# Operand slots of two sweeps, and the places of combining, norm and split, in a graph layer on one core

## The chip, the core and the metric

One NeuronCore of a Trainium2 chip runs the whole program. Time is device microseconds of one execution, as the median of three runs. The engines are TensorE (PE; PEld is its weight loading), VectorE (DVE), ScalarE (ACT), GpSimd (POOL) and SyncE (SP), which issues most DMAs. Each engine takes its instructions in the order in which they are written; semaphores join the engines.

## The reference, cut to what matters

There are 6250 nodes with 512 features and 106250 edges (50000 random pairs in both directions and a loop on each node), sorted by destination.

```python
Q = relu(x @ Wq + bq); V = x @ Wv + bv
Q = relu(layer_norm(Q)); H = sum(Q, axis=1) ** 2; H = pi / (2 * m) * H      # m from max(H) - min(H)
cosQ, sinQ = Q * cos(H), Q * sin(H)
out  = cosQ @ (cosQ.T @ V) + sinQ @ (sinQ.T @ V)
norm = cosQ @ sum(cosQ, 0) + sinQ @ sum(sinQ, 0) + EPS
gcn  = segment_sum((x @ Wg)[src] * coef, dst) + bg
y = relu(layer_norm(out / norm + gcn + V) * gamma + beta)
x = layernorm(x + y)
```

## The kernel before, in words

Nodes are cut into 49 tiles of 128 rows (`TILES`; the last, number `FULL` = 48, has 106). The program has two parts. In the first (up to about 345 us) PE multiplies every tile by Wg, and a table of rows for the graph part is written to DRAM. The second part is one list of 882 steps (`STEPS` = 49 x 18), which every engine walks with `for q in range(...)`. It is a schedule by hand: the functions `qv_at`, `cos_at`, `sin_at` and `out_at` give the step at which a tile of a stage begins, and each engine puts its share of the tile at a fixed distance `at` from there. The engines hold no common clock: an engine may be some steps ahead of another, as far as semaphores let it.

Each step holds one chunk of the graph part: POOL gathers 128 table rows by an indirect DMA (L532, a ring of 9 buffers; the gather of chunk n waits until PE is done with chunk n-9), DVE makes a 128x128 one-hot matrix (L1013, 6 buffers; it waits for the landed rows and for PE's chunk n-6), and PE multiplies the two into a bank (L1373 and L1375, the two halves of the rows). A destination tile has 18 steps; `k` is the step within it. At its end `end_tile` (L1390) announces the sum; `combine_tile` on DVE (L1043, at k = 1) adds it to the buffer `combine`; `store_combined` on ACT (L676, k = 3) writes that to DRAM; `combine_load` on SP (L415, k = 8) brings the next tile's V into the same buffer, to which `add_own` (L1023 and L1025, k = 16) adds the node's own row.

Beside the chunks run four stages, one after the other:

1. Steps 0 to 206: Q and V of 37 tiles, one tile in 6 steps. PE multiplies (L1252 to L1254: each product is made of three matmuls of high and low parts); DVE adds the biases (`v_keep` L935 at 4, `q_bias` L940 at 7) and takes the variance (L947).
2. Steps 214 to 376, the cosine sweep: cosQ.T @ V over all 49 tiles, one in 10/3 steps, summed in four banks. For tile g, ACT rounds the high parts (`m_round`: L686 for Q, L688 for V), DVE subtracts to get the low parts (`m_split`: L1094 and L1095), and PE multiplies (`m_step`). The four operands lie in a slot of the tile `operands`; there are two slots, `g % 2`, and two buffers for V's rows.
3. Steps 383 to 529, the sine sweep, one tile in 3 steps, in the same way; g runs on from 49.
4. Steps 536 to 877, the output stage, one tile in 7 steps: PE transposes Q of the next tile and multiplies it by the moments (`out_step`: products at 0 to 5, the norm sums L1491 and L1492 at 0 to 2); DVE splits the next tile's transposed Q (`o_split`, L1124) and takes the norm (`o_norm`, L1133 to L1138), both at 3, then `o_mix` (L1155, L1157) at 8, `o_affine` (L1165 to L1169) at 11, `o_factors` (L1177, L1178) at 14; ACT does `o_round` at 3, roots (L704, L707) at 10 and 13 and the last scaling (L713) at 16. Seven steps make one period, so `at` 8 stands at place 1 of the next tile's period, 11 at place 4 and 14 at place 0.

In a step DVE's one-hot stands first and the stage's work after it. PE has the opposite order:

```python
# DVE                                   # PE
chunk(seq, k)                           m_step(...) / out_step(n, at)
combine_tile(seq - 1)   # if k == 1     chunk(seq, k)
m_split(...) / o_norm(...) / o_mix(...)
```

A semaphore wait of tile n is written `done(n)`; `freed(n, 2)` is the wait for tile n-2.

## Time and profile before

| | |
|---|---|
| median of 3 runs | 1703.74 us (1702.14 to 1708.99) |
| profiled execution | 1704.63 us, its span 1702.7 us |
| PE busy | 1534.5 us (90%) |
| DVE busy | 1087.7 us (64%) |
| ACT, POOL busy | 625.4 us (37%), 922.0 us (54%) |
| granted TensorE clock, mean | 0.982 |
| DMA | 423.86 MB, 249 GB/s in the mean |

(A step of PE ends with its chunk.) Busy time is the sum of the instructions' spans on an engine. In the second part PE has no long pause; what the mean of 90% hides is where its many short pauses lie, and that is read stage by stage.

### The profile page before, as it was taken

The numbers are of one execution on the slowest core, as the hardware profiler recorded it, in microseconds if no ns is written. First come the engines' busy times: TensorE is split into PE (matmuls) and PEld (weight loads), VectorE is DVE, ScalarE is ACT, GpSimd is POOL, SyncE is SP. The second block draws the span as 40 slices with busy tenths as digits, with TensorE's granted clock in tenths as the row PEclk, the third lists the DMA queues.
The fourth block names the chain that finished last, engine by engine and source line by source line (L and its number), as shares of the span: only waits on it lengthen the run. The fifth ranks groups of instructions, "written<-read, shape, count | busy, mean of one in ns | idle before, by whom it ended". The sixth has DMA issues, their size and how long they took to land.

```text
span 1702.7 us, 24721 instructions
## 1 busy us (share of the span) xinstructions
PE 1534.5 (90%) x7715; PEld 1026.3 (60%) x7715; DVE 1087.7 (64%) x3259; ACT 625.4 (37%) x1419; POOL 922.0 (54%) x1026
## 2 busy tenths in 40 slices
PE   5788999899999898999998999989999999889995
PEld 3566777666556554655554655556666666656663
DVE  6999665655555455555555555556777777667765
ACT  5999876521212112222222222222333333233322
POOL 0000000166666666777776777776666666666662
PEclk9999999999999998999998999999999999999998
DMA  6444444698999888888787888888888888788884
GB/s 224 143 149 166 145 170 148 215 299 289 296 297 297 284 288 264 263 267 262 251 272 229 280 252 273 261 257 269 273 277 283 285 280 284 236 279 273 275 256 146
DMA packets 172757, 423.86 MB, mean 249 GB/s; under 512 B 24143, under 2 KB 25803, under 8 KB 172617
## 3 DMA queue, kind: packets, MB, share of 16 engines
q0 software_dynamic: 71120, 236.74, 45.9%
q1 hardware_dynamic: 79980, 146.16, 25.1%
q10 hardware_dynamic: 21516, 39.29, 6.0%
q8 instruction: 64, 1.05, 0.2%
q14 instruction: 77, 0.62, 0.1%
HBM read 351.42 MB, written 70.67 MB: 248 GB/s over the span
## 4 chain that ended last, share of the span: by engine, by line
PE 57%; DVE 19%; issue 10%; ACT 5%; another core or an unknown queue 3%; DMA 3%; POOL 2%; DVEq 0%; POOLq 0%; ACTq 0%; SPq 0%
PE bank L1252 12%; PE bank L1254 11%; PE bank L1253 11%; PE bank L1373 9%; PE bank L1375 8%; DVE stage L919 3%; DVE one_hot L1013 2%; DVE stage L915 2%; PE bank L1298 2%; POOL gathered L532 2%; DMA gathered<-scaled_g,index_slots 1%; DVE operands L928 1%; DVE stage L1166 1%; PE bank L1492 1%
## 5 line engine op out<-in xcount | busy, mean ns | idle before, releaser
L532 POOL DMA_INDIRECT gathered<-scaled_g,index_slots x882 | 885.6, 1004 | 420.8 <-issue 211.4
L1373 PE MATMUL bank<-gathered,one_hot 128*128 128x512 f16 x882 | 348.1, 395 | 93.8 <-DVE one_hot L1013 55.1
L1252 PE MATMUL bank<-weights,operands 128*128 128x512 f32 x784 | 396.8, 506 | 8.8 <-DVE stage L935 7.1
L1375 PE MATMUL bank<-gathered,one_hot 128*128 128x512 f16 x882 | 340.3, 386 | 0.0
L1013 DVE TENSOR_SCALAR one_hot<-iota_bf,dst_in_tile,gathered 128x128 bf16<-128x128 bf16 x882 | 257.2, 331 | 120.8 <-DMA gathered<-scaled_g,index_slots 64.5
L1253 PE MATMUL bank<-weights,operands 128*128 128x512 f32 x784 | 311.7, 398 | 0.0
L1254 PE MATMUL bank<-weights,operands 128*128 128x512 f32 x784 | 310.3, 396 | 0.0
L1373 PEld LDWEIGHTS bank<-gathered,one_hot 128*128 128x128 bf16 x882 | 85.4, 97 | 300.0 <-issue 210.8
L1252 PE MATMUL bank<-operands 128*128 128x512 f32 x392 | 198.8, 507 | 0.0
L1252 PEld LDWEIGHTS bank<-weights,operands 128*128 128x128 f32 x784 | 149.4, 191 | 72.3 <-DVE stage L935 8.8
L704 ACT ACTIVATE operands<-stage,stats 128x512 fp32r<-128x512 f32 x98 | 70.8, 723 | 328.7 <-DVE stats L1143 201.7
L517 POOL COPY dst_slots<-dst_cols 128x18 f32 x49 | 11.1, 226 | 327.0 <-issue 326.5
L686 ACT CAST operands<-nodes 128x512 fp32r<-128x512 f32 x98 | 60.7, 619 | 332.1 <-PE bank L1254 143.5
L1094 DVE TENSOR_TENSOR operands<-nodes,operands 128x512 fp32r<-128x512 f32 x98 | 68.0, 694 | 179.0 <-issue 123.3
L1254 PEld LDWEIGHTS bank<-weights,operands 128*128 128x128 f32 x784 | 148.1, 189 | 36.5
L1253 PEld LDWEIGHTS bank<-weights,operands 128*128 128x128 f32 x784 | 149.7, 191 | 22.2
L1254 PE MATMUL bank<-operands 128*128 128x512 f32 x392 | 155.2, 396 | 0.0
L1253 PE MATMUL bank<-operands 128*128 128x512 f32 x392 | 154.0, 393 | 0.0
L602 ACT ACTIVATE stage<-iota_bf,combine 128x128 bf16<-128x128 bf16 x372 | 115.8, 391 | 8.2 <-DVE combine L808 6.3
L1252 PEld LDWEIGHTS bank<-operands 128*128 128x128 f32 x392 | 74.5, 190 | 44.2 <-issue 6.0
L1375 PEld LDWEIGHTS bank<-gathered,one_hot 128*128 128x128 bf16 x882 | 88.4, 100 | 11.6 <-issue 4.0
L623 ACT ACTIVATE nodes<-nodes,stats 128x512 f32<-128x512 f32 x49 | 39.8, 812 | 142.1 <-issue 96.6
(219 smaller groups left out, 2228.0 us busy)
## 6 DMA issues: line engine op xcount, KB each, us to landing
stage<-values SPq DMA_DIRECT2D x98, 256.0 KB
stage<-in_x SPq DMA_DIRECT2D x96, 256.0 KB, 2.7
turned_x<-operands SPq DMA_DIRECT2D x37, 512.0 KB, 3.2
operands<-turned_x SPq DMA_DIRECT2D x37, 512.0 KB
gathered<-scaled_g,index_slots POOLq DMA_INDIRECT x882
scaled_g<-pairs SPq DMA_DIRECT2D x49, 260.0 KB, 2.1
pairs<-scaled_g SPq DMA_DIRECT2D x49, 260.0 KB
values<-stage ACTq DMA_DIRECT2D x49, 256.0 KB
```

Of the source, the lines that this page charges most:

```text
L532: pool.indirect_dma_start(out=plain(row_ring[k % RING]), out_offset=None, in_=table, in_offset=bass.IndirectOffsetOnAxis(ap=index_slots[:, ...
L602: last = act.activation(mod_hot[b % 2][:, HOTS + n, :], iota_bf[:, :], ACT.Sign, bias=column(stair_edge, b * STAIRS + n))
L686: act.copy(f_hi, q_tile(t))
L704: act.activation(operands[:, 5 + n % 2, :], stage[:, 2 + j, :], ACT.Square, bias=st[:, 1:2], accum_out=st[:, 2:3]).then_inc(s[f"o_squared{ ...
L919: last = dve.tensor_scalar(mod_hot[half][:, c, :], iota_bf[:, :], column(dst_mod, c0 + c), None, ALU.is_equal)
L1013: dve.tensor_scalar(one_hot[:, k % HOT, :], iota_bf[:, :], column(dst_in_tile, seq % 2 * PER_TILE + k), scale_of(row), ALU.is_equal, ALU.m ...
L1094: dve.tensor_tensor(f_lo, q_tile(t), plain(f_hi), ALU.subtract)
L1252: pe.matmul(out_ap, a_hi, b_hi, start=start and n == 0, stop=False, skip_group_check=True)
L1253: pe.matmul(out_ap, a_hi, b_lo, start=False, stop=False, skip_group_check=True)
L1254: last = pe.matmul(out_ap, a_lo, b_hi, start=False, stop=stop and n == len(pairs) - 1, skip_group_check=True)
L1373: pe.matmul(gcn_banks[seq % 2][:, :], one_hot[:, k % HOT, :], hi, start=k == 0, stop=False, skip_group_check=True)
L1375: pe.matmul(gcn_banks[seq % 2][:, :], one_hot[:, k % HOT, :], lo, start=False, stop=False, skip_group_check=True).then_inc(s["chunk_summed ...
```

## The change

Both sweeps get four operand slots, `g % 4`. Slots 2 and 3 lie in `weights[:, 2]` and `weights[:, 3]`, where V's weights stood, which no product reads after the first stage. The rows of V for them land in `pairs[:, 1]` and `pairs[:, 2]`. ACT and DVE prepare a tile two tiles ahead of PE instead of one, and SP loads V three ahead. Apart from this, `combine_tile` goes from k = 1 to 4, `store_combined` from 3 to 6, `combine_load` from 8 to 10; `o_split` and `o_norm` from 3 to 5; `o_factors` from 14 to 15; `o_last` from 16 to 17.

```diff
+        def m_parts(g):
+            slot = g % 4
+            return [operands[:, 4 * slot + n, :] if slot < 2 else weights[:, slot, n, :] for n in range(4)]
+
+        def m_values(g):
+            return stage[:, g % 4, :] if g % 4 < 2 else pairs[:, g % 4 - 1, 0:D]
...
-            def v_load(g, t):
-                sp.wait_ge(s["m_split"], freed(g, 2))
-                sp.dma_start(stage[:, g % 2, :], dram_rows(values, t, P)).then_inc(mv_loaded[g % 2], 16)
+            def v_load(g):
+                sp.wait_ge(s["m_split"], freed(g, 4))
+                sp.dma_start(m_values(g), dram_rows(values, g % TILES, P)).then_inc(mv_loaded[g % 4], 16)
...
-                if q >= 0 and k == 8:
+                if q >= 0 and k == 10:
                     sp.wait_ge(v_stored[v_slot(seq)], 16 * (v_stores_before(seq) + 1))
                     combine_load(seq)
...
-                    v_load(0, 0)
+                    for g in range(3):
+                        v_load(g)
                 for t, at in in_flight(cos_at, TILES, q):
                     if at == 0:
-                        v_load(1 + t, (1 + t) % TILES)
+                        v_load(3 + t)
...
-                act.wait_ge(s["m_summed"], freed(g, 2))
+                act.wait_ge(s["m_summed"], freed(g, 4))
                 act.copy(f_hi, q_tile(t))
...
-                if 0 < q < STEPS and seq > 0 and k == 3:
+                if 0 < q < STEPS and seq > 0 and k == 6:
                     store_combined(seq - 1)
...
-                    m_round(0, 0)
+                    m_round(0)
+                    m_round(1)
                 for t, at in in_flight(cos_at, TILES, q):
                     if at == 1:
-                        m_round((1 + t) // TILES, (1 + t) % TILES)
+                        m_round(2 + t)
...
-                    if at == out_late(n, 16):
+                    if at == out_late(n, 17):
                         o_last(n, n % 4, rows_of(n))
...
-                    if k == 1 and seq > 0:
+                    if k == 4 and seq > 0:
                         combine_tile(seq - 1)
...
-                    m_split(0, 0)
+                    m_split(0)
+                    m_split(1)
                 for t, at in in_flight(cos_at, TILES, q):
                     if at == 1:
-                        m_split((1 + t) // TILES, (1 + t) % TILES)
+                        m_split(2 + t)
...
-                    if at == 3 and n < FULL:
+                    if at == 5 and n < FULL:
                         o_split(n + 1, (n + 1) % 2)
-                    if at == 3:
+                    if at == 5:
                         o_norm(n, n % 2)
...
-                    if at == out_late(n, 14):
+                    if at == out_late(n, 15):
                         o_factors(n, n % 4)
```

The sine sweep is changed in the same way as the cosine sweep. The order of the instructions follows from it. First DVE in the output stage, one period of seven steps before the change; L1124 is the split, L1133 to L1138 the norm, L1165 to L1143 the affine part, L1013 the one-hots:

```order
L1124 TENSOR_TENSOR operands<-bank,operands 128x512
L1133 ISA stats<-bank,cos_sin 128x4
L1133 ISA stats 128x1
L1137 RECIPROCAL stats<-stats 128x1
L1138 TENSOR_SCALAR stats<-cos_sin,stats 128x2
L1013 TENSOR_SCALAR one_hot<-iota_bf,dst_in_tile,gathered 128x128
L1165 RECIPROCAL stats<-stats 128x1
L1166 SCALAR_TENSOR_TENSOR stage<-stage,stats,bias 128x512
L1167 SCALAR_TENSOR_TENSOR stage<-stage,stats,bias 128x512
L1169 SCALAR_TENSOR_TENSOR stage,stats<-stage 128x512
L1143 TENSOR_SCALAR stats<-stats 128x1
```

and the same place of the changed kernel, where the split is L1131, the norm L1140 to L1145, the affine part L1172 to L1150 and the one-hots L1022:

```order
L1172 RECIPROCAL stats<-stats 128x1
L1173 SCALAR_TENSOR_TENSOR stage<-stage,stats,bias 128x512
L1174 SCALAR_TENSOR_TENSOR stage<-stage,stats,bias 128x512
L1176 SCALAR_TENSOR_TENSOR stage,stats<-stage 128x512
L1150 TENSOR_SCALAR stats<-stats 128x1
L1022 TENSOR_SCALAR one_hot<-iota_bf,dst_in_tile,gathered 128x128
L1131 TENSOR_TENSOR operands<-bank,operands 128x512
L1140 ISA stats<-bank,cos_sin 128x4
L1140 ISA stats 128x1
L1144 RECIPROCAL stats<-stats 128x1
L1145 TENSOR_SCALAR stats<-cos_sin,stats 128x2
L1022 TENSOR_SCALAR one_hot<-iota_bf,dst_in_tile,gathered 128x128
```

Split and norm have gone from ahead of the affine part to behind it, and the one-hot of place 5 now stands between them.

Second, DVE at the start of a destination tile in the first stage, before the change (L955 to L940 are Q's factors and bias, L947 to L935 the variance and V's bias, L1043 is the combining):

```order
L1013 TENSOR_SCALAR one_hot<-iota_bf,dst_in_tile,gathered 128x128 x2
L1043 SCALAR_TENSOR_TENSOR combine<-bank,dinv,combine 128x512
L955 RECIPROCAL stats<-stats 128x1
L956 SCALAR_TENSOR_TENSOR stats<-stats 128x1
L940 TENSOR_TENSOR nodes<-bank,bias 128x512
L1013 TENSOR_SCALAR one_hot<-iota_bf,dst_in_tile,gathered 128x128 x3
L947 BN_STATS bn_parts<-nodes 128x6
L948 BN_AGGR stats<-bn_parts 128x2
L935 TENSOR_TENSOR stage<-bank,bias 128x512
```

and of the changed kernel, where the combining is L1052:

```order
L1022 TENSOR_SCALAR one_hot<-iota_bf,dst_in_tile,gathered 128x128 x2
L964 RECIPROCAL stats<-stats 128x1
L965 SCALAR_TENSOR_TENSOR stats<-stats 128x1
L949 TENSOR_TENSOR nodes<-bank,bias 128x512
L1022 TENSOR_SCALAR one_hot<-iota_bf,dst_in_tile,gathered 128x128 x3
L1052 SCALAR_TENSOR_TENSOR combine<-bank,dinv,combine 128x512
L956 BN_STATS bn_parts<-nodes 128x6
L957 BN_AGGR stats<-bn_parts 128x2
L944 TENSOR_TENSOR stage<-bank,bias 128x512
```

The combining has moved behind three more one-hots, and ahead of the variance and V's bias.

Third, DVE ahead of the cosine sweep, before the change (L1085 splits the angles, L1094 and L1095 are one tile's split):

```order
L1085 TENSOR_TENSOR cs<-cos_sin,cs 128x49x2
L1013 TENSOR_SCALAR one_hot<-iota_bf,dst_in_tile,gathered 128x128
L1094 TENSOR_TENSOR operands<-nodes,operands 128x512
L1095 SCALAR_TENSOR_TENSOR operands<-stage,cos_sin,operands 128x512
L1013 TENSOR_SCALAR one_hot<-iota_bf,dst_in_tile,gathered 128x128
```

and of the changed kernel, where they are L1094, L1101 and L1102:

```order
L1094 TENSOR_TENSOR cs<-cos_sin,cs 128x49x2
L1022 TENSOR_SCALAR one_hot<-iota_bf,dst_in_tile,gathered 128x128
L1101 TENSOR_TENSOR operands<-nodes,operands 128x512
L1102 SCALAR_TENSOR_TENSOR operands<-stage,cos_sin,operands 128x512
L1101 TENSOR_TENSOR operands<-nodes,operands 128x512
L1102 SCALAR_TENSOR_TENSOR operands<-stage,cos_sin,operands 128x512
L1022 TENSOR_SCALAR one_hot<-iota_bf,dst_in_tile,gathered 128x128
```

A second tile is split there; from then on each split stands where it stood, and is that of the tile after.

## Rows read from the trace of the kernel before

**Rows 1.** Windows of the stages: us; PE, PEld, DVE, ACT, POOL busy; PEclk, DMA share, GB/s.

```profile
345.00:655.00 310.00, 287.78 (x1237) 178.92 (x1237) 162.48 (x468) 63.35 (x143) 201.47 (x234) 0.99 0.89 290
668.00:908.00 240.00, 231.33 (x1015) 138.15 (x1013) 125.21 (x294) 60.04 (x96) 172.10 (x182) 1.00 0.83 261
922.00:1138.00 216.00, 205.34 (x888) 128.06 (x887) 116.90 (x271) 59.18 (x94) 156.48 (x165) 0.99 0.85 268
1151.00:1675.00 524.00, 484.53 (x2422) 338.67 (x2421) 383.09 (x1216) 166.59 (x377) 349.73 (x388) 0.99 0.86 272
```

**Rows 2.** Waits of DVE in 668:908: line <- releaser: us, times, longest.

```profile
DVE operands L1094 <- issue: 65.1, 29, 4.3
DVE operands L1094 <- ACT operands L688: 26.5, 14, 4.1
```

**Rows 3.** Timeline of PE, ACT and DVE in 860:868: start, us [idle before].

```profile
860.69 0.40 PE L1254 MATMUL bank<-operands 128*128 128x512 f32 x1
...
864.95 0.62 ACT L686 CAST operands<-nodes 128x512 fp32r<-128x512 f32 x1 [7.15 <-remote]
...
866.23 0.69 DVE L1094 TENSOR_TENSOR operands<-nodes,operands 128x512 fp32r<-128x512 f32 x1 [4.18 <-issue]
...
867.87 0.39 PE L1373 MATMUL bank<-gathered,one_hot 128*128 128x512 f16 x1 [2.21 <-DVE one_hot L1013]
```

**Rows 4.** Waits of DVE in the first stage, 345:655.

```profile
DVE one_hot L1013 <- DMA gathered<-scaled_g,index_slots: 48.4, 43, 3.4
...
DVE combine L1043 <- remote: 28.2, 6, 5.1
```

**Rows 5.** Timeline of PE and DVE in 553:561, around one combining.

```profile
553.51 0.17 PE L1390 MATMUL bank<-zero_bf 128*128 128x8 bf16 x1
...
558.96 0.75 DVE L1043 SCALAR_TENSOR_TENSOR combine<-bank,dinv,combine 128x512 f32<-128x512 f32 x1 [5.13 <-remote]
...
560.85 0.39 PE L1373 MATMUL bank<-gathered,one_hot 128*128 128x512 f16 x1 [1.98 <-issue]
```

**Rows 6.** Timeline in 1326:1332: PE's chunks at places 2, 4, 5, 6, then DVE.

```profile
1326.18 0.39 PE L1373 MATMUL bank<-gathered,one_hot 128*128 128x512 f16 x1
...
1329.16 0.39 PE L1373 MATMUL bank<-gathered,one_hot 128*128 128x512 f16 x1
...
1331.79 0.39 PE L1373 MATMUL bank<-gathered,one_hot 128*128 128x512 f16 x1 [1.32 <-issue]
...
1332.23 0.38 PE L1373 MATMUL bank<-gathered,one_hot 128*128 128x512 f16 x1
...
1327.47 0.69 DVE L1124 TENSOR_TENSOR operands<-bank,operands 128x512 fp32r<-128x512 f32 x1 [1.21 <-ACT operands L699]
1328.08 0.15 DVE L1133 CUSTOM_DVE_ANT_1 stats<-bank,cos_sin 128x4 f32<-128x4 f32 x1
...
1328.61 0.31 DVE L1013 TENSOR_SCALAR one_hot<-iota_bf,dst_in_tile,gathered 128x128 bf16<-128x128 bf16 x1
...
1329.02 0.75 DVE L1166 SCALAR_TENSOR_TENSOR stage<-stage,stats,bias 128x512 f32<-128x512 f32 x1
...
1331.42 0.76 DVE L1013 TENSOR_SCALAR one_hot<-iota_bf,dst_in_tile,gathered 128x128 bf16<-128x128 bf16 x3
```

**Rows 7.** Waits of DVE in the output stage, 1151:1675.

```profile
DVE combine L1043 <- remote: 17.5, 7, 4.2
```

**Rows 8.** Window over the pause at 1461.84, columns as in the first group.

```profile
1459.00:1467.00 8.00, 5.16 (x17) 3.66 (x18) 6.43 (x19) 2.94 (x8) 3.18 (x4) 0.57 0.82 255
```

**Rows 9.** Waits of POOL in the output stage, 1151:1675.

```profile
POOL gathered L532 <- PE bank L1375: 83.9, 81, 2.9
```

**Rows 10.** Timeline of DVE and SP near the end, 1660:1680.

```profile
1663.98 0.75 DVE L1043 SCALAR_TENSOR_TENSOR combine<-bank,dinv,combine 128x512 f32<-128x512 f32 x1 [0.28 <-issue]
...
1668.75 0.32 SPq L426 DMA_DIRECT2D stage<-gcn_plus_values  x1
...
1675.19 0.75 DVE L1155 SCALAR_TENSOR_TENSOR stage<-bank,stats,stage 128x512 f32<-128x512 f32 x1 [0.77 <-issue]
```

47 lines of the change are left out of this document (23 added, 24 removed).

## The prediction, as it was put on record

> **What bounds the kernel now.** I read the page first: PE is the busiest engine. Then the busy time of each stage in windows, since a mean over stages with different limits says little. The first part has no edit in it, so its 345 us stay. In the second part PE is busy for 287.8 of 310 us, 231.3 of 240, 205.3 of 216 and 484.5 of 524 [rows 1]: it stands idle for 22.2, 8.7, 10.7 and 39.5 us. These are the places where time can be won; a stage cannot become shorter than PE's busy time in it, while its instructions stay as they are. No other engine is near its limit: in the output stage DVE is busy for 73% and POOL for 67%.
>
> Next I read what stands ahead of each pause on PE, in its timeline and DVE's. The pauses lie ahead of a chunk whose one-hot is late, and the one-hot is late because DVE, which works in written order, stood at a wait for PE. In the sweeps the wait is that of L1094, 65.1 + 26.5 = 91.6 us in the cosine sweep [rows 2]. One case: the last matmul of the group that frees a slot ends by the trace at 860.69 + 0.40 = 861.09; ACT begins to round into the slot at 864.95, DVE splits at 866.23, and PE gets its one-hot at 867.87, after 2.21 us of nothing [rows 3]. So ACT started 3.9 us after the trace's end of what it waited for. The same is seen in the first stage: L1390 ends at 553.68, the combining that waits for it starts at 558.96, 5.3 us later, and PE pauses for 1.98 us [rows 5]. A signal from PE may thus arrive up to 5 us late, and a wait placed close behind PE's work pays for it. Whether a wait costs something is then a matter of how many steps lie between the work and the wait.
>
> The Trainium skill has a rule that reads this otherwise (Perfetto Trace Analysis, Tensor Engine Instruction): a matmul's end in the profile is estimated, and its semaphore is pushed only when PSUM acknowledges the bytes. By it, PE would still be at work in those 5 us and the pauses would be smaller than they look; what that makes of the time is the third rival below. The row fits either reading: the 5.3 us are there, and the matmuls that the trace puts behind 553.68 would fill them.
>
> **The change part by part.**
>
> *Four slots.* Nothing is added: as many copies, splits and loads, each one tile earlier. Before, the split of tile g stands one step behind the first products of g-1 and needs the last ones of g-2: that is 10/3 + 1 - 2 = 2.3 steps after them, some 2.3 x 240/163 = 3.4 us. ACT needs 1.3 us of that before DVE can start (864.95 to 866.23), so a signal more than about 2 us late makes DVE wait. With four slots it needs the last products of g-4 and stands 5.7 steps or 8.3 us behind them. A lateness of 3.9 to 5.3 us is covered, and ACT's 1.3 us with it. What is late next: the gathered rows, which bind DVE in the first stage for 48.4 us [rows 4], and the one-hot's own wait for the chunk six back. Of the 8.7 + 10.7 = 19.4 us of idle PE in both sweeps I take 14 us; bounds 8 (DVE still meets landing rows) and 18.
>
> *Combining at k = 4.* Its wait for L1390 gets three steps more, 3 x 310/207 = 4.5 us. In the first stage six such waits cost DVE 28.2 us [rows 4]; by the ratio of the one case (1.98 of 5.13) PE lost up to 10.9 us, and I take 8 as there, since shorter waits leave less. Against it: the 0.75 us of L1043 now stand ahead of the variance and V's bias, in a step after which PE takes two chunks with nothing between them. In some 10 tiles of this stage that may cost up to 0.75 us each, 7.5 in all; half of it is covered where DVE waits for V's product anyway. Net gain 4 us; bounds -3 and 8. In the output stage the seven waits of 17.5 us [rows 7] go into the next term.
>
> *Norm and split at 5.* The norm waits for PE's norm sums of place 2. From PE's chunk at place 2 to that at place 5 there are 1331.79 - 1326.18 = 5.6 us, less the 1.32 of pause: 4.3 us [rows 6]. In the same time DVE has, from the norm's start at 1328.08: norm, one-hot, affine part, one-hot, with PE's start at 1331.79: 3.7 us. So 0.6 us of lateness is all that is free, and each further one is a pause, once per tile: 39.5 us over 48 tiles is 0.8 us each. After the change only the norm (0.53 us) and one one-hot (0.37) stand between this wait and PE's chunk at place 6, for which PE takes 4.3 + 0.44 us: 3.8 us of lateness are free. What is next: the affine part (2.4 us from 1329.02 to 1331.42), a one-hot 0.3, split 0.6, norm 0.5 and one-hot 0.4 now form 4.2 us of work between the one-hots of places 4 and 6, while PE needs 1.3 + 0.44 = 1.7 us (2.63 less the pause, and 1331.79 to 1332.23). DVE must be 2.5 us ahead at place 4. It can be: its whole work is 383.1/48 = 8.0 us a tile against PE's 484.5/48 = 10.1 us, and its earlier wait (the mixing, for the products of place 5) is some 9 us of PE's work ahead of the next place 4, of which DVE's own work there (two factors, a mixing of two 0.75 us instructions, three one-hots) takes 3 us. That leaves 6 us less the lateness: enough up to 3.5 us of it. The own-row addition (two instructions like L1166, 1.5 us) and the combining (0.75 us), each once in 18 steps, use up the rest where they fall together. I take 24 of the 39.5 us; bounds 8 and 34. Later factors and last scaling are off PE's path: the slots of the output rows are four, and one step later frees them in time.
>
> *The clock.* Around the pause of 3.0 us at 1461.84 the granted clock is 0.57 over 8 us [rows 8]: (1 - 0.57) x 8 = 3.4 us of full clock lost. In the sine sweep and the output stage the mean is 0.99 [rows 1], 2.2 and 5.2 us lost by that. With the pauses gone the clock stays at 2.4 GHz instead of falling to 1.2: I take 5 us, bounds 0 and 7. The dips at the angles and behind each sweep stay, since DVE's serial work there is untouched.
>
> *The ends.* Ahead of the cosine sweep DVE splits a second tile (1.44 us) and ACT rounds one more; this stands on the way to the first products: 0 to 1.4 us lost. At the end, tile 47 is combined three steps later. Now the combining at 1663.98, its store, and the load at 1668.75 are followed by the mixing at 1675.19, which waits 0.77 us [rows 10]; there is no room, and three steps are 3 x 1.4 = 4.2 us, less what DVE runs further ahead. Both together -3 us; bounds -6 and 0.
>
> Sum: 14 + 4 + 24 + 5 - 3 = 44 us. From the profiled execution's 1704.6 us (span 1702.7 and 1.9 around it; 0.9 above the median shown) that gives **1660 us**, by the median 1659.7.
>
> **The rivals.**
>
> *Signals grow later when PE never pauses.* A pause lets PE's signals catch up. If lateness goes to 5 us everywhere, the norm's 3.8 us and the mixing's margin no longer suffice, and half of the pauses come back: output 12, sweeps 10, the rest as above with 2 for the clock: 25 us, 1679 us. For it: the first stage, where 5 us are seen. Against: in the output stage the waits listed are shorter, 4.2 us at most [rows 7]. Chance 0.2.
>
> *The gathers become the bound.* POOL waits 83.9 us for PE in the output stage [rows 9] and is busy 1.04 us per step of 1.56; DMA moved 272 GB/s there and 290 in the first stage [rows 1]. At 290 the output stage could shrink to 524 x 272/290 = 491 us, by 33: above my 24. This caps the gain and lies inside the range; with gathers later still, 1672 us. It counts with the forecast.
>
> *The pauses are none.* If PE works off a backlog during the 5 us, only pauses longer than the lateness count, and nearly all are shorter. Then nothing moves but the ends: 1704.6 + 3 - 5 = 1702 us. It is the page's rule put to work. Against: PE's chunk at 1331.79 follows at once on its one-hot, begun at 1331.42 and 0.31 us long, as if nothing else had to be done first [rows 6]. Chance 0.12.
>
> *Slower: the long block of DVE.* If DVE does not get 2.5 us ahead at place 4, PE waits there in every tile. Today its one-hot of place 4 is there 0.24 us before PE (1328.61 + 0.31 against 1329.16). The change breaks even on this stage where the lead stays at 2.5 - 0.8 = 1.7 us. At a lead of 1.0 us the pause is 1.5 us, 72 us over 48 tiles, 33 more than now; with the other terms (+20) that is 1717 us. For it: today's lead. Against: today's lead is what the norm's wait leaves, and that wait goes behind the block. Chance 0.08.
>
> **How the numbers follow.** The forecast (1640 to 1678 us) has 0.6, the first rival 0.2 (1672 to 1692), no effect 0.12, slower 0.08. A measurement of this kernel tells 0.5%, 8.5 us, from no change, so the border to faster is 1695.2: faster 0.79, same 0.12, slower 0.09. The range holds forecast and first rival: 1640 to 1692 us.
>
> **What would show it.** In the sweeps L1094's successor (the split) should hardly wait, PE should be busy in over 97% of both; the waits should move to one-hots, for landed rows or for PE's chunk six back. In the output stage the pauses at place 5 should go, and what is left stand at places 4 and 6, where own rows or combining fall in. The combining should wait for less than 10 us in all. The granted clock should be 1.00 through the sine sweep and the output stage. Wrong would be: PE's idle time as before under another name, above all ahead of the one-hot of place 6; or a PE without pauses at an unchanged span.

## The result, and the profile after the change

The changed kernel takes **1698.4 us** (median of 16 runs, 1688.8 to 1704.9); the kernel before takes 1706.9 us beside it (16 runs, 1701.5 to 1712.8). The ratio is 0.9953, with a 95% interval of 0.9939 to 0.9967, clear of 1: by the ratio 8 us gained, where 44 had been predicted. The time lies outside the range (1640 to 1692 us), and 8 us is less than the 0.5% that the prediction called faster. The profiled execution took 1700.5 us, its span 1698.7.

The windows of the four stages after the change, for [rows 1] (columns as there; the bounds are again those of the stages):

```profile
345.00:655.00 310.00, 289.88 (x1242) 179.94 (x1240) 161.27 (x460) 62.29 (x142) 201.73 (x233) 0.99 0.88 290
669.00:908.00 239.00, 233.17 (x1020) 138.71 (x1018) 129.53 (x301) 58.28 (x94) 170.59 (x181) 1.00 0.84 260
921.00:1138.00 217.00, 209.43 (x896) 129.62 (x895) 116.90 (x269) 55.79 (x90) 157.58 (x165) 0.98 0.83 261
1156.00:1668.00 512.00, 482.20 (x2422) 334.69 (x2423) 382.88 (x1214) 167.72 (x377) 345.99 (x386) 1.00 0.87 276
```

The first stage and the sweeps are as long as they were (310, 239 and 217 us against 310, 240 and 216). Only the output stage is shorter, by 12 us, and PE still stands idle for 30 us in it. Summed from PE's records between the chunks that bound each stage, its pauses are:

| stretch | before: length, pauses | after: length, pauses |
|---|---|---|
| first stage | 312.5, 23.2 | 313.6, 21.6 |
| cosine sweep | 241.3, 8.7 | 239.3, 6.0 |
| sine sweep | 216.3, 10.7 | 216.5, 8.2 |
| sine sweep to output stage | 12.4, 4.8 | 18.1, 10.4 |
| output stage | 524.6, 39.5 | 512.3, 29.8 |
| last chunks | 10.3, 1.3 | 12.8, 3.6 |

What the edits were aimed at did happen. The wait of DVE for the split, 91.6 us in the cosine sweep [rows 2], is almost gone (its largest entry there is now 10.8 us). But DVE waits nearly as long at other instructions: from 345 to 1680 us its waits add up to 483 us, before the change to 493. These are the largest waits of DVE from 345 to 1680 us after the change (engine, line, releaser: us in total, times, longest):

```profile
DVE one_hot L1022 <- DMA gathered<-scaled_g,index_slots: 236.4, 183, 4.0
DVE one_hot L1022 <- issue: 79.4, 110, 4.2
DVE one_hot L1022 <- PE bank L1383: 40.7, 34, 3.4
DVE stage L1162 <- remote: 19.2, 14, 3.1
```

In the output stage the pauses moved by one place. Ahead of place 5 they fell from 28.1 us (28 pauses) to 4.1 us (6); ahead of place 6 they grew from 2.6 us (5) to 18.0 us (19). A further 5.0 us (14) stand at place 3, where there were none; most of them lie between products that wait for nothing the trace shows, and why is open.

The 19 pauses at place 6 are of three kinds, by what DVE last waited for ahead of the late one-hot. Seven (8.8 us) stand right behind the norm's wait. Nine (6.0 us) stand behind a block of some 4.5 us in which DVE works without a stop, from the one-hot of place 4 or from the affine part ahead of it. In three (3.0 us) a one-hot had waited for PE's chunk six back. Here is one of the first kind in the timeline of PE and DVE after the change (start, us, engine, line, operation [idle before <- releaser]):

```profile
1241.32 0.25 PE L1502 MATMUL bank<-sums,operands 128*128 128x2 f32 x1
...
1243.98 0.68 DVE L1131 TENSOR_TENSOR operands<-bank,operands 128x512 fp32r<-128x512 f32 x1
...
1245.33 0.39 PE L1262 MATMUL bank<-weights,operands 128*128 128x512 f32 x1
...
1246.29 0.16 DVE L1140 CUSTOM_DVE_ANT_1 stats<-bank,cos_sin 128x4 f32<-128x4 f32 x1 [1.63 <-remote]
...
1246.83 0.31 DVE L1022 TENSOR_SCALAR one_hot<-iota_bf,dst_in_tile,gathered 128x128 bf16<-128x128 bf16 x1
...
1247.20 0.39 PE L1381 MATMUL bank<-gathered,one_hot 128*128 128x512 f16 x1 [1.03 <-DVE one_hot L1022]
```

The last norm-sum matmul of place 2 ends at 1241.57. The norm, although three steps behind it now, starts at 1246.29, 4.7 us later, and PE pauses for 1.03 us. The prediction had counted 3.8 us of lateness as free.

The trace also records the semaphore events themselves. In this place six signals of PE arrive in a row:

```
PE instruction ends (us)                      its signal arrives
1241.57  norm sums, place 2                   1246.27
1242.04, 1243.88, 1245.02  chunks 594 to 596  1246.31, 1246.41, 1246.47
1245.72  last product                         1246.53
1246.17  chunk 597                            1246.57
```

Work that PE's records spread over 4.6 us is signed off within 0.3 us. The signals are held back and then come together, in order. The Trainium skill (Perfetto Trace Analysis, Tensor Engine Instruction) says that a matmul's end in the profile is an estimate and that its signal goes out when PSUM has acknowledged the bytes. The row agrees in that end and signal differ, here by 4.7 us.

With these events the lateness can be measured for all kernels (signal minus the end of its matmul; the median of the logged signals, chunks left out). In the part of the kernel in which no gather runs, up to 330 us, it is 0.01 us before and after. Further on, with the number of signals that are recorded:

```
                  before            after
first stage       2.2 (70 of 81)    1.5 us (59 of 81)
cosine sweep      0.3 (45 of 59)    1.1    (40 of 59)
sine sweep        0.5 (40 of 58)    1.4    (39 of 59)
output stage      0.1 (106 of 166)  2.0    (141 of 166)
norm sums alone   0.2 (33 of 48)    2.3    (48 of 48)
```

Signals that are missing from the record don't make this difference. A norm can't start ahead of its signal, and in the kernel before, over all 48 tiles, it starts in the median 0.17 us behind the end of its sums. DVE's and ACT's own signals, as far as they are recorded, come 0.01 us behind their instructions in 90% of cases on this chip too; it is PE's that are late.

The time at which lateness begins and ends goes with the gathers. In this trace and in those of the five other kernels on this chip, each recorded PE signal ahead of the first gather comes within 0.02 us. The first late one belongs to a matmul that ends 9.0 to 9.9 us behind the start of the first gather, and from 2 us behind the last gather on none is over 0.4 us late. That is a coincidence in time; it doesn't show which of the two makes the other, or what else begins there.

In the output stage and the sweeps, where the change moved waits away from signals, the signals became later; in the first stage, where it moved the combining, they did not. At the border behind the sine sweep one late signal is seen to cost more. The sweep ends with DVE waiting for the last product, which by the trace ends at 1136.76 + 0.40:

```profile
1136.76 0.40 PE L1262 MATMUL bank<-operands 106*128 106x512 f32 x1
...
1143.74 2.72 DVE L1121 SCALAR_TENSOR_TENSOR stage<-bias,moment_sums,bank 128x512 f32<-128x512 f32 x4 [5.05 <-remote]
...
1149.75 0.61 PE L1381 MATMUL bank<-gathered,one_hot 128*128 128x512 f16 x1 [10.40 <-DVE one_hot L1022]
```

DVE starts 6.6 us after that end, and the pause at this border is 10.4 us, where it was 4.8. So in this trace what the two sweeps gained (2.7 and 2.5 us of pauses) is given back at the border behind them.

### The profile page after: what moved, and what is told of

Its sections match the earlier page's. It is cut to its first block, busy times and chain, and to the rows that moved or that the text cites. A ratio compares the mean times of both kernels' runs of the same rounds, so it can differ in the third digit from the quotient of the medians.

```text
span 1698.7 us, 24721 instructions
## 1 busy us (share of the span) xinstructions
PE 1539.6 (91%) x7715; PEld 1024.7 (60%) x7715; DVE 1092.4 (64%) x3259; ACT 625.2 (37%) x1419; POOL 921.5 (54%) x1026
## 4 chain that ended last, share of the span: by engine, by line
PE 53%; DVE 15%; issue 10%; DMA 9%; POOL 5%; ACT 5%; another core or an unknown queue 2%; POOLq 0%; SPq 0%; DVEq 0%; ACTq 0%
PE bank L1260 11%; PE bank L1261 11%; PE bank L1262 11%; PE bank L1381 8%; PE bank L1383 8%; DMA gathered<-scaled_g,index_slots 5%; POOL gathered L541 5%; DVE stage L928 3%; DVE stage L924 2%; DMA scaled_g<-pairs 2%; DVE one_hot L1022 1%; ACT stage L611 1%; DVE operands L937 1%; PE bank L1306 1%
## 5 line engine op out<-in xcount | busy, mean ns | idle before, releaser
L1022 DVE TENSOR_SCALAR one_hot<-iota_bf,dst_in_tile,gathered 128x128 bf16<-128x128 bf16 x882 | 269.0, 327 | 360.7 <-DMA gathered<-scaled_g,index_slots 236.4
L1261 PE MATMUL bank<-weights,operands 128*128 128x512 f32 x784 | 312.5, 399 | 1.3 <-issue 1.2
L1260 PE MATMUL bank<-operands 128*128 128x512 f32 (+1 forms) x200 | 101.6, 508 | 0.0
L1260 PE MATMUL bank<-weights 128*128 128x512 f32 x192 | 97.5, 508 | 0.0
L1383 PEld LDWEIGHTS bank<-gathered,one_hot 128*128 128x128 bf16 x882 | 88.5, 100 | 10.7 <-issue 4.9
L694 ACT CAST weights<-nodes 128x512 fp32r<-128x512 f32 x48 | 29.7, 618 | 174.4 <-PE bank L1262 69.4
L694 ACT CAST operands<-nodes 128x512 fp32r<-128x512 f32 x50 | 30.9, 618 | 151.5 <-PE bank L1262 57.7
L721 ACT ACTIVATE stage<-stage,stats 128x512 f32<-128x512 f32 (+1 forms) x49 | 40.0, 816 | 122.8 <-issue 66.5
L1260 PE MATMUL bank<-gathered,operands 128*128 128x512 f32 (+1 forms) x196 | 85.0, 434 | 0.0
L928 DVE TENSOR_SCALAR stage<-iota_bf,nodes 128x128 bf16<-128x128 bf16 x465 | 83.4, 247 | 0.0
```

The costliest lines, as they stand in the source:

```text
L694: act.copy(f_hi, q_tile(t))
L721: act.activation(z, z, ACT.Identity, scale=stats[0:r, j, 3:4], bias=stats[0:r, j, 4:5])\
L928: last = dve.tensor_scalar(mod_hot[half][:, c, :], iota_bf[:, :], column(dst_mod, c0 + c), None, ALU.is_equal)
L1022: dve.tensor_scalar(one_hot[:, k % HOT, :], iota_bf[:, :], column(dst_in_tile, seq % 2 * PER_TILE + k), scale_of(row), ALU.is_equal, ALU.m ...
L1260: pe.matmul(out_ap, a_hi, b_hi, start=start and n == 0, stop=False, skip_group_check=True)
L1261: pe.matmul(out_ap, a_hi, b_lo, start=False, stop=False, skip_group_check=True)
```

## The experiments

**One part of the change at a time, and a deeper ring, on the first chip.** Three kernels have one part of the change each; the fourth adds a tenth buffer for gathered rows to the changed kernel. The main lines of their edits, in this order (store and load go with the combining, factors and last scaling with norm and split, as in the change):

```diff
 slots_only: after.py with the places of before
-if k == 4 and seq > 0: combine_tile(seq - 1)
+if k == 1 and seq > 0: combine_tile(seq - 1)
-if at == 5: o_norm(n, n % 2)      # and the split
+if at == 3: o_norm(n, n % 2)
 norm_split_5: before.py
-if at == 3: o_norm(n, n % 2)      # and the split
+if at == 5: o_norm(n, n % 2)
-if at == 3 and n < FULL: o_round(n + 1, (n + 1) % 2)    # ACT
+if at == 5 and n < FULL: o_round(n + 1, (n + 1) % 2)
-if at == out_late(n, 14): o_factors(n, n % 4)
+if at == out_late(n, 15): o_factors(n, n % 4)
 combine_4: before.py
-if k == 1 and seq > 0: combine_tile(seq - 1)
+if k == 4 and seq > 0: combine_tile(seq - 1)
 ring10: after.py
-RING = 9
+RING = 10    # row_ring = 9 of gathered + [pairs[:, 3, :]], chunk n uses n % RING
```

`norm_split_5` is not quite the part alone: it also moves ACT's rounding `o_round` from 3 to 5, which the changed kernel leaves at 3.

> The kernel before with the four operand slots alone; combining, norm and split stand where they stood. The whole change gave 8 us. Theory A, the ring of gathered rows: with the slots DVE no longer waits for L1094, but a gather may only be issued when PE has signed off the chunk nine back, so DVE now stands at the one-hots for landed rows instead; the two sweeps give their 5 us of pauses in the trace (8.7 + 10.7 to 6.0 + 8.2) and lose them again where the sine sweep ends (the pause there went from 4.8 to 10.4 us): 0 to -3 us. Theory B, PE was behind and not idle: pauses shorter than the lateness of its signals hid work still to be done, so nothing at all can be won in the sweeps: 0 to +2 us, and the pause behind the sine sweep is again some 10 us. If either forecast of the prediction were right for this part it would be -14 us.

> The kernel before with only the output stage changed: norm and split at place 5, factors and last scaling one place later. In the whole change the output stage went from 524.6 to 512.3 us, its pauses from 39.4 to 29.3: those at place 5 from 28 to 4 us, those at place 6 from 3 to 18. Both theories expect -8 to -12 us, nearly the whole gain; if the combining has a share in it, -5 to -8.

> The kernel before with only the combining moved from k = 1 to k = 4 (with its store and its load). In the whole change the first stage did not become shorter (310.7 to 311.6 us): six pauses of 1.3 to 1.7 us ahead of the chunk k = 2 went, and seven of 1.0 to 2.7 us ahead of k = 5 came. Expected: 0 us in the first stage, 0 to -3 in the output stage, where the combining's wait of 17.5 us for seven tiles goes. The prediction's term was -4.

> The changed kernel with a tenth buffer in the ring of gathered rows (in a buffer that lies idle by then), nothing else: a gather may be issued one step, 1.4 to 1.5 us, earlier. Theory A (the gathers, which wait for PE's late signals, hold DVE back): landed rows stand 1.5 us more ahead of the one-hots, the 236 us that DVE waits for landed rows fall to under 120, and the pauses at place 6 of the output stage and in the sweeps shrink: -6 to -12 us against the changed kernel, ratio to the kernel before 0.989. Theory B (PE behind, not idle): the waits of DVE fall just the same, but the time stays within 3 us of the changed kernel's, ratio 0.994 to 0.996.

Measured, beside a kernel before of 1705.8 us:

| kernel | median us | ratio, 95% interval |
|---|---|---|
| slots_only | 1703.5 | 0.9987 (0.9969 to 1.0005) |
| norm_split_5 | 1703.7 | 0.9985 (0.9967 to 1.0003) |
| combine_4 | 1704.5 | 0.9990 (0.9975 to 1.0005) |
| ring10 | 1696.8 | 0.9945 (0.9924 to 0.9966) |

No part alone can be told from no change; by the medians they add up to 5.7 us. The expectation that norm and split would give nearly the whole gain (8 to 12 us) failed on this chip: 2.1 us (-0.5 to 5.6). Slots gave 2 us against the 14 predicted; the pause at the border behind the sine sweep was 8.4 us in that trace, as in ring10's (the changed kernel 10.4; without slots 4.8, 4.8 and 7.1 in three traces). Combining moved its pauses in the first stage from k = 2 to k = 5 (22.3 us in all, before 23.2).

The parts are not independent in the output stage. With norm and split moved and the combining still at k = 1, 13.2 us of pauses stay at place 5, and 11.0 of them stand behind the combining's wait for a late signal. This is the largest group of DVE's waits in that stage (1152 to 1670 us):

```profile
DVE combine L1043 <- remote: 28.6, 8, 5.2
```

And one trace tells lengths only roughly here. In the kernels whose output stage is the old one or has the combining alone moved, it is 524.6 us (before), 519.1 (slots) and 520.1 us (combining) long, with 39.5, 35.9 and 35.2 us of pauses; with norm and split moved it is 518.0 (alone), 512.3 (the whole change) and 512.6 us (ring10), with 30.2, 29.8 and 26.8. So the 12 us by which it became shorter above may hold some 5 us of scatter.

The tenth buffer did to DVE what was expected. Its waits for landed rows from 345 to 1680 us fell from 236.4 us to

```profile
DVE one_hot L1022 <- DMA gathered<-scaled_g,index_slots: 114.8, 97, 4.3
```

while the ratio went from 0.9953 to 0.9945, 1.4 us, with intervals that overlap. By these intervals the buffer gives 6 us at most, of the 36 that are missing. Late gathers are thus not what most of the expected gain was lost to. A time that stays while the waits fall (0.994 to 0.996) is what the other reading had expected, PE behind its trace and not idle; the run doesn't part it from signals that grow later. Nor do the slots alone: 2.3 us less, with this interval, fits both. What went elsewhere is seen in the lateness of the norm sums' signal in the output stage, in all six kernels: 0.2 us before, 0.1 with slots only, 0.4 with the combining alone, 1.6 with norm and split alone, 2.3 after, 2.7 with the tenth buffer. In the cosine sweep the lateness is 0.3 us before, 0.2 with the combining alone, 0.0 with norm and split alone, 1.3 with the slots alone. In the sine sweep it scatters more: 0.5, 1.0, 0.0, and 1.5 with the slots alone.

**Without waits for rows, without gathers, and a better order: another chip.** Two kernels take the gathered rows out of the chain; two more try to turn the remaining pauses into time.

```diff
 rows_unused: after.py
-row = plain(row_ring[k % RING])
+row = still                       # pairs[:, 3, :], set to 1.0 once; PE reads it too
-pool.wait_ge(s["chunk_summed"], freed(chunk_number(seq, k), RING))
+pool.wait_ge(s["chunk_hot"], freed(chunk_number(seq, k), RING))
+pool.wait_ge(landed[k % RING], 16 * (chunk_number(seq, k) // RING))
-dve.wait_ge(landed[k % RING], ...)
+dve.wait_ge(s["still_set"], 1)
 no_gathers: rows_unused
-pool.indirect_dma_start(out=plain(row_ring[k % RING]), ...).then_inc(landed[k % RING], 16)
+pool.sem_inc(landed[k % RING], 16)
 norm_6: after.py
-if at == 5: o_norm(n, n % 2)
+if at == 6: o_norm(n, n % 2)
 combined_best: norm_6 with RING = 10 and
-if k == 4 and seq > 0: combine_tile(seq - 1)
+if k == 3 and seq > 0: combine_tile(seq - 1)
-if ... k == 6: store_combined(seq - 1)
+if ... k == 5: store_combined(seq - 1)
```

In the first two, engines that compute wait for no row; POOL alone waits until the gather nine back has landed.

> The changed kernel, in which one-hots and chunk matmuls read one fixed buffer of ones instead of the gathered rows (so the sums over neighbours are left out of the output); the gathers are still issued, as many bytes to the same ring, but paced by the one-hot nine back and no longer by PE's signal, and nobody waits for their landing. Theory A (late gathers hold the kernel): with the 236 us of waits for landed rows gone, half or more of PE's 87 us of pauses go: 1650 to 1670 us. Theory B (PE is behind its trace; the pauses in it are mostly made up): the pauses shrink, the lateness of PE's signals grows in their place (in the output stage from a median of 2.3 us for the norm's), and the time stays at 1685 to 1700 us.

> The kernel of the run before with the gathers themselves left out (POOL only signals), so 237 of 424 MB of DMA traffic and POOL's work go (sums over neighbours are left out of the output). If the lateness of PE's signals comes of the gathers' traffic or of POOL's work, it falls to under 0.5 us, as in the first part of the kernel where no gather runs, and with it the pauses: 1610 to 1640 us. If it is PE's own, lateness and time are those of the run before within 5 us: 1680 to 1700 us.

> The changed kernel with the norm of the output stage one place later still, at 6 (the split stays at 5). After the change 19 pauses stand ahead of place 6, 18 us in all, some of them behind the norm's wait for PE, up to 1.9 us. Theory of the prediction (each wait far enough behind its signal returns its pause): -6 to -12 us against the changed kernel, ratio to the kernel before 0.989 to 0.992. Theory B (PE behind): pauses at place 6 fall, the signals' lateness grows, time within 3 us of the changed kernel's: 0.994 to 0.997.

> The changed kernel with the norm at 6, the combining at k = 3 (a step in which DVE has nothing of V's product or variance, where at k = 4 it has both) and the tenth buffer of gathered rows. If pauses in the trace can still be turned into time, the three together give -8 to -15 us against the changed kernel: ratio to the kernel before 0.986 to 0.990. If PE is behind, they add little to the 1.5 us of the tenth buffer: 0.992 to 0.996.

| kernel | median us | ratio, 95% interval |
|---|---|---|
| before | 1620.7 | |
| rows_unused | 1607.9 | 0.9918 (0.9898 to 0.9938) |
| no_gathers | 1605.6 | 0.9905 (0.9885 to 0.9925) |
| norm_6 | 1610.6 | 0.9937 (0.9921 to 0.9953) |
| combined_best | 1607.8 | 0.9914 (0.9899 to 0.993) |

The surprise stands in the first line: the same kernel before takes 85 us less here. These runs fell on another chip. The absolute times expected above were made for the first one and say nothing here, so that the kernels had to be read against a trace of before and after from such a chip:

> The kernel before once more, for its trace. On a chip without late signals PE's pauses in the output stage should be under 10 us (on the first chip 39.5) and in the sweeps under 3 (19.4), so that there was little for the change to win; what it wins there must come from fixed places: the wait for a combining, a split or a norm that lies too close behind its product even with prompt signals. On a chip with late ones: the trace of [rows 1] again within 2 us a stage.

> The changed kernel once more, unchanged. In the last four runs, on another chip, the kernel before took 1620.7 us instead of 1705.8, the changed one with the norm at 6 took 1610.6, and no signal of PE was late there (all within 0.04 us of the matmul's end; PE never paused in the output stage); on the first chip signals came up to 7 us late. On a chip without late signals: 1608 to 1613 us, no pauses in sweeps and output, the gain 8 to 11 us. On a chip with them: 1698 us, pauses of some 87 us, the gain 8 us.

The kernel before took 1621.2 us there, and the changed one 1611.7 beside 1620.2, a ratio of 0.9946 (0.9932 to 0.9959). The windows of the four stages of the kernel before on this chip, for [rows 1]:

```profile
346.00:636.00 290.00, 285.61 (x1245) 180.39 (x1245) 163.60 (x471) 61.56 (x141) 205.39 (x236) 0.99 0.94 313
646.00:878.00 232.00, 231.68 (x1025) 139.26 (x1023) 124.03 (x294) 59.85 (x96) 170.89 (x184) 1.00 0.86 271
891.00:1095.00 204.00, 203.08 (x894) 127.74 (x893) 117.65 (x272) 59.39 (x95) 157.08 (x167) 1.00 0.88 283
1107.00:1592.00 485.00, 475.68 (x2420) 335.35 (x2419) 384.94 (x1215) 166.25 (x377) 350.69 (x388) 1.00 0.90 294
```

and of the changed kernel:

```profile
344.00:635.00 291.00, 286.19 (x1247) 180.59 (x1245) 163.62 (x472) 63.28 (x141) 205.28 (x236) 0.99 0.93 312
646.00:878.00 232.00, 231.68 (x1026) 139.40 (x1024) 129.43 (x302) 59.21 (x95) 171.94 (x184) 1.00 0.86 274
890.00:1094.00 204.00, 203.35 (x895) 127.86 (x893) 117.62 (x271) 56.40 (x91) 159.58 (x167) 1.00 0.88 280
1105.00:1580.00 475.00, 473.56 (x2422) 336.24 (x2423) 380.83 (x1215) 166.22 (x377) 355.95 (x389) 1.00 0.91 300
```

On this chip no logged signal of PE came more than 0.04 us late, in any stage of either kernel. Before the change PE had 0.3 us of pauses in the cosine sweep, 0.9 in the sine sweep and 9.3 in the output stage; the first chunk starts at 346 us as on the first chip (345). So the 85 us between the chips lie wholly in the stages in which gathers run. In the two traces 67 us of them are pauses and 17 us are longer busy time of PE for the same matmuls, 9 of these in the output stage (484.5 against 475.7 us). What makes that busy time longer isn't shown; the granted clock is 0.99 and 1.00 there.

Of the 9.3 us in the output stage the change takes 7.9. The pauses stand at place 5 where the own rows fall together with the affine part. Here is one in the timeline of DVE and PE of the kernel before, on this chip:

```profile
1208.19 0.16 DVE L1133 CUSTOM_DVE_ANT_1 stats<-bank,cos_sin 128x4 f32<-128x4 f32 x1 [0.50 <-PE bank L1492]
...
1208.95 0.75 DVE L1023 SCALAR_TENSOR_TENSOR combine<-pairs,own_scale,combine 128x512 f32<-128x512 f16 x1
...
1210.60 0.75 DVE L1166 SCALAR_TENSOR_TENSOR stage<-stage,stats,bias 128x512 f32<-128x512 f32 x1
...
1213.05 0.31 DVE L1013 TENSOR_SCALAR one_hot<-iota_bf,dst_in_tile,gathered 128x128 bf16<-128x128 bf16 x1
...
1213.41 0.39 PE L1373 MATMUL bank<-gathered,one_hot 128*128 128x512 f16 x1 [1.10 <-DVE one_hot L1013]
```

From the norm to the late one-hot, DVE works without a stop for 4.9 us, and PE waits 1.1 us for it. With the norm's and the split's waits behind this block, it may start ahead. The waits of DVE in the sweeps, 646 to 1094 us, first of the kernel before, then of the changed one, say the rest:

```profile
DVE operands L1094 <- ACT operands L688: 175.6, 90, 4.6
```

```profile
DVE one_hot L1022 <- DMA gathered<-scaled_g,index_slots: 165.3, 139, 3.9
```

DVE waited for 175.6 us at the splits, and PE lost 1.2 us by it. The four slots exchanged this wait for one of 165.3 us at the landed rows, and the sweeps kept their length to within 0.4 us. A wait on an engine with time to spare is no loss, however long.

At the end the change loses. Tile 47 is combined later, and the own rows of the last tile wait for the load behind its store; the pause ahead of the last chunk is 4.0 us (before 1.1). The own rows' timeline in the changed kernel:

```profile
1591.20 0.75 DVE L1032 SCALAR_TENSOR_TENSOR combine<-pairs,own_scale,combine 128x512 f32<-128x512 f16 x1 [2.91 <-DMA combine<-values]
```

The two kernels that use no gathered rows ran again there:

> The changed kernel that gathers but doesn't wait for the rows (sums over neighbours are left out of the output), once more. On a chip with late signals: what gathers cost through their landing alone goes, what they cost as traffic stays: 1650 to 1670 us if the landing is what counts, 1685 to 1700 us if the late signals of PE do. On a chip without: 1608 us again.

> The changed kernel without gathers (sums over neighbours are left out of the output), once more. On a chip with late signals: if the lateness comes of the gathers' traffic or POOL's descriptors, it goes, and with it PE's pauses: 1605 to 1615 us, as on the chip without late signals. If it has nothing to do with them, 1680 to 1700 us. On a chip without late signals: 1605.6 us again.

They gave 1607.1 (0.9921) and 1606.5 us (0.9916), and the waits and traffic of 237 MB of gathers are thus worth 5 us on such a chip, against the changed kernel. Without the waits but with the traffic it is 4.5 us.

**What can be won at all, and a third and a fourth chip.** To `combined_best` this kernel adds the last tile's combining at its old place:

```diff
 best2: combined_best
-if k == 3 and seq > 0: combine_tile(seq - 1)
+if k == (3 if seq < FULL else 1) and seq > 0: combine_tile(seq - 1)
-if ... k == 5: store_combined(seq - 1)
+if ... k == (5 if seq < FULL else 3): store_combined(seq - 1)
```

> The changed kernel with the norm at 6, the combining at k = 3, ten buffers for gathered rows, and in the last tile the combining back at k = 1, so that its store, the load and the own rows of the last tile are in time: on the chip without late signals the kernel with the first three had 2.2 us of pauses left at the end. Without late signals 1605 to 1607 us, ratio to the kernel before 0.990 to 0.992. With late signals 1690 to 1697 us, 0.990 to 0.995; 0.985 if pauses can be turned into time there.

> The changed kernel that gathers but waits for no row (sums over neighbours are left out of the output). On a chip with late signals: 1685 to 1698 us and lateness of 2 to 6 us if PE's signals are late through the traffic; 1605 to 1615 us if they are not late without the wait for rows. On a chip without: 1607 us again.

> The changed kernel without gathers (sums over neighbours are left out of the output), once more. On a chip where PE's signals come late while the gathers run: if the lateness comes of the gathers' traffic or of POOL's descriptors, it is gone here and the time is 1605 to 1615 us; if it is the chip's own and has nothing to do with them, lateness as before and 1680 to 1700 us. On a chip without late signals: 1606 us again.

It takes 1606.9 us beside 1619.8, a ratio of 0.9916 (0.9903 to 0.993): 12.8 us less than the kernel before, as fast as the kernel that leaves the rows unused (1607.0) and 1.6 us behind the one without gathers (1605.3). Its sine sweep and output stage:

```profile
890.00:1092.00 202.00, 202.00 (x892) 127.56 (x890) 117.33 (x268) 56.17 (x91) 157.31 (x167) 1.00 0.88 283
1104.00:1577.00 473.00, 473.00 (x2421) 336.60 (x2420) 380.87 (x1218) 166.14 (x377) 350.84 (x389) 1.00 0.92 302
```

PE is busy for all of it. What remains is PE's own work, with 18 us of pauses: 4.2 in the first stage, 3.0 at the angles, 5.8 and 4.8 at the borders behind the sweeps. `combined_best` itself was 1607.8 us, so the last edit is worth less than can be measured, though its trace has no pause left at the end (2.2 us before it). This kernel wasn't run on the first chip.

> The kernel before with norm and split of the output stage at place 5, and factors and last scaling one later, nothing else, once more. On a chip without late signals the output stage of the whole change went from 485.7 to 475.4 us and no other stage moved: -9 to -11 us, ratio 0.993 to 0.9945, the whole gain. If combining or slots had a share in it there: -3 to -7 us. On a chip with late signals: 0.9985 again.

Norm and split alone take 1609.3 us beside 1620.7, 0.9933 (0.992 to 0.9947), and the output stage's pauses are 1.6 us. That is at least what the whole change gives (0.9946; the intervals overlap). If the other parts cost something, it is at the end: the pause ahead of the last chunk is 0.6 us here and 4.0 with the combining moved.

> The changed kernel without gathers (sums over neighbours are left out of the output), once more, for a chip with late signals: 1605 to 1615 us and prompt signals if the lateness comes of the gathers, 1680 to 1700 us if not. On a chip without late signals: 1606 us.

> The changed kernel without gathers (sums over neighbours are left out of the output), a last time, for a chip with late signals: 1605 to 1615 us if the lateness comes of the gathers, 1680 to 1700 us if not. On a chip without late signals 1606 us, and the cause of the late signals stays open.

Both fell on a chip with prompt signals (1606.1 and 1604.5 us). In all, 14 runs fell on three chips on which the kernel before takes 1619.8 to 1620.7 us, and four on the first chip, whose times and late signals are those of the runs of the result. None of the runs without gathers met late signals, so their question, whether the lateness comes of the gathers, is not answered.

## Why the prediction was wrong

**What bounds the kernel.** Right: PE, and the time to be won is PE's pauses, behind one-hots that are late because DVE met a late signal. The trace of the second chip shows it: with prompt signals the pauses of the kernel before are 29 us instead of 96 (from the first chunk on), and this is most of the 85 us between the chips. The step that failed is the next one: "Whether a wait costs something is then a matter of how many steps lie between the work and the wait." The lateness was taken as a fixed size, 3.9 to 5.3 us at most, that distance covers. It isn't fixed. Where the waits were moved back, the lateness in the output stage rose from 0.1 to 2.0 us in the median and reached 7.9. So the distance that was bought was used up in part: where the parts ahead of the clock counted 42 us, PE's pauses fell from 96.1 to 87.6 us.

**Four slots, 14 us.** Measured 2.3 us alone on the first chip (interval -0.9 to 5.3), and no more than 1.2 us to win where signals are prompt. The split's wait went, as said. The sweeps gained 5.2 us of pauses together, and 5.6 came back at the border behind the sine sweep in that trace (3.6 in the one of the slots alone). The sum had no term for the border. That the gathers are late next was named, and true; the tenth buffer shows that it cost little.

**Combining at k = 4, 4 us.** Measured 1.3 us alone (-0.9 to 4.3). In the first stage the gain was eaten where the prediction had named a cost (L1043's 0.75 us in the same step as the variance): pauses went from k = 2 to k = 5. What the move is worth lies in the output stage, beside the norm's: without it, 11.0 us of pauses stay behind the combining's wait. With prompt signals its trace shows only the cost, some 3 us at the end.

**Norm and split, 24 us.** This term was mis-sized most. Alone the part gave 2.1 us on the first chip (-0.5 to 5.6) and 11 on another (8.6 to 13). In the traces of the whole change the output stage became 12.3 us shorter on the first chip, of which some 5 may be scatter, and 10.3 on the second. Place 5 behaved as predicted (28.1 to 4.1 us), and the 3.8 us of free lateness at place 6 is where it failed: 13 of 48 signals of the norm sums came later than that, against 2 of the 33 recorded before. Seven pauses, 8.8 us in all, stand behind the norm's wait; one is that shown above, where the signal was 4.7 us late. The long block, named as a rival (DVE not ahead at place 4), came true in a small part only: not in every tile, but in nine pauses at place 6, 6.0 us in all, each behind some 4.5 us of DVE's work.

**The clock, 5 us.** The output stage ran at 1.00 as predicted (before 0.99), the sine sweep at 0.98 (before 0.99). Falls of the clock like the one at 1461.84 before [rows 8] were gone from the output stage, but the stretch at 1.2 GHz behind the sine sweep lasted 13.7 us instead of 6.8. Over the span the mean granted clock went from 0.982 to 0.979. No gain. The lengths of these stretches scatter: 3.4 to 13.7 us behind the sine sweep in six traces.

**The ends, -3 us.** Right: 2.5 us lost at the end in the first chip's trace, 2.6 in the second's.

**The rivals.** The first, signals that grow later when PE does not pause, is nearest to what was seen; it was given 0.2 and priced at 25 us, three times what came. Its price assumed that lateness stops at 5 us. That signals grew later in the output stage is shown; that PE's missing pauses are the reason is not. The third (no effect, 1702 us) was nearest in time, in part by a slip: it lets nothing move but the ends, which cost 3 us, and then takes off 5 us that are the clock's term. By its own words it gives 1707.6 us. Its mechanism is not shown and has one observation against it: a backlog would be worked off one matmul after another, while six signals for 4.6 us of recorded work came within 0.3 us. The run that was to decide it, without waits for rows, never fell on the first chip. The gathers as the bound, counted with the forecast, find no support: half of DVE's wait for their rows went for 1.4 us, and leaving them out entirely is worth 5 us where that could be measured, with prompt signals.

What holds PE's signals back on the first chip is open. It begins within 10 us of the first gather and ends with the last; whether the gathers cause it wasn't tried there, because later runs fell on other chips. That the signals of a stage come later where its waits were moved back is shown by six kernels for the output stage and the cosine sweep, on one chip; why, is not.

## What to carry to other kernels

A wait of 175 us on an engine with spare time may be worth nothing: ask what PE lost by it before moving it, and count only PE's pauses, at the borders of the stages too, where a gain inside is easily given back. Lateness of a signal is not a constant of the kernel or of the chip's kind: price an edit that rests on it for both cases, late and prompt, and run the same kernel on a second chip before explaining a few tens of microseconds. Try a moved wait in a step in which its engine has nothing else. Look at parts together, too: a second wait close behind a late signal can keep the pauses that the first one's move was to take.

## What the runs showed of the hardware

- Two chips of one kind differ by 85 us in 1706 for the same kernel: signals of PE arrive within 0.04 us on one (and on two more), and up to 7.9 us late on another. There the first late one belongs to a matmul that ends 9 to 10 us behind the first gather, and 2 us behind the last gather none is over 0.4 us late (0.01 us ahead of the gathers). The signals of DVE and ACT are not late (0.01 us).
- In the place shown, late signals come together and in order: six within 0.3 us for work recorded over 4.6 us.
- On the chip with late signals, the same matmuls of the output stage are recorded as busy for 482 to 488 us in six traces, on the others for 473 to 476, with 0.98 to 1.00 of the clock granted on the first and 1.00 on the second.
- 236.7 MB of gathers beside the matmuls cost the latter nothing on the chips with prompt signals: PE is busy for the full 473 us of the output stage in the kernel with the gathers (473.4 us from its first to its last chunk) and in the one without (473.5).
